# Maxima of attention scores for two heads at once on row tiles of 64 partitions, and the value projection as one product of 128 columns

## What is computed

```python
h = h + attn(layernorm(h))        # 64 images, 861 tokens, 4 heads of 16
h = h + ffn(layernorm(h))         # a shared MLP and the two best of four experts

# attn
q, k, v = heads(x @ Wq.T + bq), heads(x @ Wk.T + bk), heads(x @ Wv.T + bv)
attn = softmax(einsum('bhnd,bhmd->bhnm', q, k) * 16 ** -0.5)
out = einsum('bhnm,bhmd->bhnd', attn, v)
```

## Time and profile before

| | us |
|---|---|
| median of 3 runs | 5057.14 (5054.25 to 5059.23) |
| profiled execution | 5066.99 |
| its span, first to last instruction | 5065.2 |
| PE busy in the span | 4809.6 |
| DVE busy in the span | 3530.6 |
| ACT busy in the span | 2990.7 |

### The profile page before, as it was taken

The page is one execution under the profiler, slowest core; times in us unless marked ns, Lnnn a source line. Parts: engine busy times, 40 slices in busy tenths (PEclk is TensorE's granted clock), DMA queues, the critical chain, the costliest instruction groups (busy, mean ns, idle before and its releaser), DMA issues.

```text
span 5065.2 us, 81302 instructions
## 1 busy us (share of the span) xinstructions
PE 4809.6 (95%) x29710; PEld 3201.2 (63%) x29710; DVE 3530.6 (70%) x7660; ACT 2990.7 (59%) x6161; POOL 1272.2 (25%) x1169
## 2 busy tenths in 40 slices
PE   6699999999999999999999999999999999999997
PEld 5466666666666666666656666666666666666654
DVE  4477667777777777777677777777767677777774
ACT  0156566666566566566656556666656666656665
POOL 3122222222222222223222222222223222222221
PEclk8699999999999999999999999999999999999998
DMA  2433323333433332333332333332333333332220
GB/s 87 106 72 76 85 78 78 85 71 76 87 79 78 85 73 78 86 81 77 84 70 75 84 80 78 86 72 74 87 83 79 80 82 71 79 85 69 40 47 6
DMA packets 193397, 386.00 MB, mean 76 GB/s; under 512 B 74986, under 2 KB 118634, under 8 KB 193002
## 3 DMA queue, kind: packets, MB, share of 16 engines
q1 hardware_dynamic: 191978, 379.91, 33.3%
q10 hardware_dynamic: 1024, 0.89, 0.1%
HBM read 309.13 MB, written 109.26 MB: 83 GB/s over the span
## 4 chain that ended last, share of the span: by engine, by line
PE 55%; issue 23%; POOL 10%; DVE 6%; ACT 3%; DMA 2%; POOLq 0%; SPq 0%; ACTq 0%; DVEq 0%; another core or an unknown queue 0%
PE ps L1225 9%; PE ps L1204 8%; PE ps L1213 8%; PE ps L1257 8%; PE ps L1275 5%; PE ps L1248 4%; PE ps L1318 3%; DVE neg_max_halves L977 3%; POOL tokens L829 3%; POOL moe_T L824 2%; ACT probs L861 2%; PE ps L1339 2%; PE ps L364 1%; POOL nodes_T L806 1%; DMA image_rows<-image_by_row 1%
## 5 line engine op out<-in xcount | busy, mean ns | idle before, releaser
L977 DVE TENSOR_REDUCE neg_max_halves<-ps 123x1 f32<-123x432 f32 (+1 forms) x3584 | 2014.6, 597 | 602.6 <-PE ps L1225 592.9
L861 ACT ACTIVATE probs<-ps 123x432 f32<-123x432 f32 x3584 | 1684.0, 541 | 603.3 <-PE ps L1204 580.4
L1225 PE MATMUL ps<-k_stack,q_stack 96*123 96x432 f32 x3584 | 1302.3, 397 | 35.7 <-DMA k_stack<-qk_scratch 21.6
L1204 PE MATMUL ps<-q_stack,k_stack 97*123 97x432 f32 x3584 | 1246.8, 394 | 63.9 <-DVE neg_max_halves L977 22.1
L1225 PEld LDWEIGHTS ps<-k_stack,q_stack 96*123 96x123 f32 x3584 | 646.7, 188 | 431.6 <-issue 290.3
L1204 PEld LDWEIGHTS ps<-q_stack,k_stack 97*123 97x123 f32 x3584 | 642.8, 186 | 359.0 <-issue 96.2
L1213 PE MATMUL ps<-probs,v_and_one 123*32 123x432 f32 x7168 | 787.8, 553 | 14.0 <-ACT probs L861 14.0
L924 ACT ACTIVATE hidden<-ps,plain_w 128x432 f32<-128x432 f32 x640 | 400.2, 634 | 181.0 <-PE ps L1275 180.9
L1257 PE MATMUL ps<-adjacency,parts_hi 112*128 112x392 f32 x1344 | 466.1, 347 | 5.1 <-DVE parts_lo L999 4.1
L1257 PE MATMUL ps<-adjacency,parts_lo 112*128 112x392 f32 x1344 | 459.9, 342 | 0.0
L359 POOL COPY patch_columns<-image_rows 96x392 f32<-96x392 f32 x256 | 243.2, 978 | 845.0 <-PE ps L364 756.2
(11 more groups left out here) (157 smaller groups left out, 6115.3 us busy)
## 6 DMA issues: line engine op xcount, KB each, us to landing
image_rows<-image_by_row SPq DMA_DIRECT2D x256, 586.9 KB
q_stack<-qk_scratch SPq DMA_DIRECT2D x256, 216.0 KB, 7.9
k_stack<-qk_scratch SPq DMA_DIRECT2D x256, 216.0 KB, 9.3
image_by_row<-in_x SPq DMA_DIRECT2D x192, 196.0 KB
qk_scratch<-parts_hi SPq DMA_DIRECT2D x64, 432.0 KB, 2.5
qk_scratch<-parts_lo SPq DMA_DIRECT2D x64, 432.0 KB, 3.1
out<-tokens SPq DMA_DIRECT2D x64, 215.2 KB
tokens_next<-in_txt SPq DMA_DIRECT2D x64, 19.2 KB
```

Of the source, the lines that this page charges most:

```text
L861: act.activation(P[:, (g * 2 * NB + unit) % SLOTS, h, :], T[0:BLK, 0:HW], ACT.Exp, scale=SCALE).then_inc(free[r], 1)
L977: v.tensor_reduce(NM[:, qb * HEADS + h, half:half + 1], T[0:BLK, 0:keys], AX.X, ALU.max, negate=True).then_inc(free[r], 1)
L1204: mm = pe.matmul(T[0:BLK, 0:cn], KS[:, g % 2, h, kb * BLK:(kb + 1) * BLK], QS[:, g % 2, h, c0:c0 + cn], start=True, stop=True)
L1225: mm = pe.matmul(T[0:BLK, 0:cn], QS[0:SHIFT_ROW, g % 2, h, qb * BLK:(qb + 1) * BLK], KS[0:SHIFT_ROW, g % 2, h, c0:c0 + cn], start=True, st ...
```

## The change

- The query and key stacks of heads 0 and 1 stay in rows 0 to 63 (shift row 96). Those of heads 2 and 3 move to rows 64 to 127, with rows 0 to 63 zero but for their shift row, which is row 0.
- `mx` contracts over 64 rows at tile position (0, 0) for heads 0 and 1 and (64, 0) for heads 2 and 3. Four of them share one time in the list: heads h and h+2 of the first half of the keys, then h and h+2 of the second. The list has 14 such groups for each image in place of 56 single steps. The number of matmuls and of VectorE reductions is the same.
- `s` contracts over 97 rows for heads 0 and 1 and over 128 for heads 2 and 3.
- The stacks are filled by 16 transfers of two heads each, in place of 8 of four. The maxima's row goes out in two transfers, in place of one, each time.
- `v` has one product of 128 columns for each block (high and low weights side by side, `vsplit`), in two steps of 4 and 3 blocks, and VectorE adds bias and both parts in two additions for each step: four in place of one for each image.
- The table of times is changed in many places by up to a few hundredths of a period.

```diff
-STACK_PARTS = 8
+STACK_PARTS = 16
...
-        for h in range(HEADS):
-            for half in range(2):
-                out.append(("mx", g, qb, h, half))
-                out += due[:1] if half else []
-                due = due[1:] if half else due
+        for h in range(2):
+            out.append([("mx", g, qb, h + up, half) for half in range(2) for up in (0, 2)])
+            out += due[:1]
+            due = due[1:]
...
-MAX = ((-0.693, 0.158), (-0.638, 0.167))
+MAX = ((-0.691, 0.196), (-0.631, 0.174))
...
-VALUE = (-1.012, -0.998)
+VALUE = (-0.962, -1.061)
...
-                        copy, part, keys = n // 4, n // 2 % 2, n % 2
-                        src = scratch[b, part, keys].rearrange("h r c -> r h c")
-                        at = HD * (2 * part + copy) if keys else HD * (2 * copy + part)
+                        copy, part, keys, upper = n // 8, n // 4 % 2, n // 2 % 2, n % 2
+                        hs = slice(2 * upper, 2 * upper + 2)
+                        src = scratch[b, part, keys, hs].rearrange("h r c -> r h c")
+                        at = 64 * upper + (HD * (2 * part + copy) if keys else HD * (2 * copy + part))
...
-                        act.dma_start(QS[SHIFT_ROW:SHIFT_ROW + 1, g % 2, :, c].bitcast(F32), MR[:, c].bitcast(F32)).then_inc(mrow_dma[part], 16)
+                        for hs, at in ((slice(0, 2), SHIFT_ROW), (slice(2, 4), 0)):
+                            act.dma_start(QS[at:at + 1, g % 2, hs, c].bitcast(F32), MR[hs, c].bitcast(F32)
+                                          ).then_inc(mrow_dma[part], 16)
...
-                        v.tensor_tensor(
-                            VV[:, b, :, :, 0:HD],
-                            T[0:BLK, 0:NB * HID].rearrange("p (k h d) -> p k h d", h=HEADS, d=HD),
-                            row("bv").rearrange("p (h d) -> p h d", h=HEADS).unsqueeze(1)
-                            .to_broadcast([BLK, NB, HEADS, HD]), ALU.add).then_inc(free[r], 1)
+                        two = T[0:BLK, 0:kn * 2 * HID].rearrange("p (k a h d) -> p k a h d", a=2, h=HEADS, d=HD)
+                        bias = row("bv").rearrange("p (h d) -> p h d", h=HEADS).unsqueeze(1).to_broadcast([BLK, kn, HEADS, HD])
+                        done(v.tensor_tensor(VV[:, g % 2, k, :, 0:HD], two[:, :, 0, :, :], bias, ALU.add), st)
+                        need(st)
+                        v.tensor_tensor(VV[:, g % 2, k, :, 0:HD], two[:, :, 1, :, :], VV[:, g % 2, k, :, 0:HD], ALU.add
+                                        ).then_inc(free[r], 1)
...
-                        mm = pe.matmul(T[0:BLK, 0:cn], KS[:, g % 2, h, kb * BLK:(kb + 1) * BLK],
-                                       QS[:, g % 2, h, c0:c0 + cn], start=True, stop=True)
+                        k = SHIFT_ROW + 1 if h < 2 else 128
+                        mm = pe.matmul(T[0:BLK, 0:cn], KS[0:k, g % 2, h, kb * BLK:(kb + 1) * BLK],
+                                       QS[0:k, g % 2, h, c0:c0 + cn], start=True, stop=True)
...
-                        mm = pe.matmul(T[0:BLK, 0:cn], QS[0:SHIFT_ROW, g % 2, h, qb * BLK:(qb + 1) * BLK],
-                                       KS[0:SHIFT_ROW, g % 2, h, c0:c0 + cn], start=True, stop=True)
+                        at = 64 * (h // 2)
+                        mm = pe.matmul(T[0:BLK, 0:cn], QS[at:at + 64, g % 2, h, qb * BLK:(qb + 1) * BLK],
+                                       KS[at:at + 64, g % 2, h, c0:c0 + cn], start=True, stop=True, tile_position=(at, 0))
...
-                            for part in (WH, WL):
-                                mm = pe.matmul(T[0:BLK, k * HID:(k + 1) * HID], x_, wsplit(part, "v"),
-                                               start=part is WH, stop=part is WL)
+                    elif kind == "v":
+                        for k, at in blocks_of(st[2]):
+                            mm = pe.matmul(T[0:BLK, at * 2 * HID:(at + 1) * 2 * HID],
+                                           XS["a"][:, k * BLK:(k + 1) * BLK], vsplit[:, :], start=True, stop=True)
```

More of the change, by code:

```diff
@@ L746, in run @@
                 landed(stack_dma, 16, "stack")
-                landed(mrow_dma[0], 16, "mload", 0)
-                landed(mrow_dma[1], 16, "mload", 1)
+                landed(mrow_dma[0], 32, "mload", 0)
+                landed(mrow_dma[1], 32, "mload", 1)
             def end(n):
@@ L886, in run @@
                         act.wait_ge(full[r], n)
-                        counted(act, mrow_dma[part], row_no[part], ("mload", st[1] - 1, part), 16)
+                        counted(act, mrow_dma[part], row_no[part], ("mload", st[1] - 1, part), 32)
                         act.activation(blocked(MR[:, c0:c0 + cn]), pitched(T[0:HEADS, :], cn),
```

70 lines of the change are left out of this document (37 added, 33 removed).

## The result

| | before | after |
|---|---|---|
| median of the runs, us | 5058.2 (4 runs) | 5445.9 (5436.5 to 5451.9, 4 runs) |
| profiled execution, us | 5067.0 | 5440.4 |

The ratio is 1.0763, 95% interval 1.0740 to 1.0786: 7.6% slower. The forecast was 5013, with 8 chances in 10 between 4880 and 5150. It named slower as possible, through rival (b), at 5146; what came lies over four times as far from the kernel before as that.

What follows compares the result with a forecast made beforehand. It took TensorE's own work to bound the kernel, beside it VectorE emptying banks where maxima are dense; 5067 - 154 + 98 + 8 + 4 = 5023 us profiled, 5013 for the median, 8 in 10 between 4880 and 5150.

Steps and rivals of the forecast that it cites:

- rival (b): At reuse of a group's four banks, VectorE's bursts decide: waits at the upper end, +231 us, 5146 us, slower; chance 0.25.
- Products side by side, 0.40 for a group: In the maxima's products, row tiles run in pairs, 0.40 us for four instead of 0.80: 353 us saved.
- the switches, 0.19 each: On TensorE, each change of tiling costs 0.19 us, array running empty plus exposed first load: 1301 of them, 247 us lost.
- (a): On TensorE, the first load after a switch is hidden and banks cost nothing new: 4834 us; chance 0.17.
- (c): In the maxima's groups, loads of row tiles go one after another: +97 us, 5110 us; chance 0.08.
- (d): In the maxima's groups, row tiles run one after another, so the 353 us saving is lost: 5268 us; chance 0.05.
- Value projection, -48: In the value products, 7 products per step group cost as much each as 14 did: 48 us saved; VectorE's additions counted nothing.
- What is late next, the banks, +98, at most +231: At the PSUM banks, groups fill four of six, so TensorE waits for VectorE's reductions: 309 us replacing 211, at most 442.
- My walk through the list: Over the changed order of steps, 584 of 896 groups ask for banks too early, by 0.53 us on average: 309 us.
- TensorE's gain of 154: TensorE's own work falls by 353 for paired products, less 247 for switches, plus 48 for value products: 154 us.
- Transfers, +8 and +4: Doubled issues for the maxima's row on ScalarE's queue cost 8 us (0 to 76); extra stack transfers cost 4 us.
- The cover that I named for the stacks: Stack transfers land in 8.9 us and start some 20 us ahead of the first `mx`: hidden, except for the first image.

Runs made afterwards that it cites:

- full rows in fours: The kernel before with only the maxima's products put in groups of four, on full rows (96) without row tiles: 5574.3 us, ratio 1.1013.

## Why the prediction was wrong, by its steps

- **Products side by side, 0.40 for a group, and the switches, 0.19 each: right.** From the changed kernel with short reductions and exponentials, two untiled products, a group and two more, where nothing is waited for:

```profile
3017.32 0.47 PE L1291 MATMUL ps<-x_stack_moe,split_hi 128*128 128x432 f32 x1
3017.63 0.35 PE L1291 MATMUL ps<-x_stack_moe,split_lo 128*128 128x432 f32 x1
3017.91 0.66 PE L1241 MATMUL ps<-k_stack,q_stack 64*123 64x432 f32 x4
3018.51 0.46 PE L1291 MATMUL ps<-x_stack_moe,split_hi 128*128 128x432 f32 x1
3018.80 0.36 PE L1291 MATMUL ps<-x_stack_moe,split_lo 128*128 128x432 f32 x1
```

  and its loads:

```profile
3017.91 0.29 PEld L1241 LDWEIGHTS ps<-k_stack,q_stack 64*123 64x123 f32 x4 [0.29 <-issue]
3018.50 0.19 PEld L1291 LDWEIGHTS ps<-x_stack_moe,split_hi 128*128 128x128 f32 x1 [0.30 <-issue]
```

  From 3017.63 to 3018.80 are 1.17 us, where my terms give 0.29 + 0.30 + 0.29 + 0.30 = 1.18 and six starts without tiles 1.20. Inside a group, the medians over the 754 that start at full clock are 3 ns from the first to the second start, 294 to the third and 3 to the fourth. This rules out (a), (c) and (d), each by its own sign: the first load after a switch is exposed, loads of row tiles don't go one after another, and the tiles do run together. It also says how little an isolated group had to give: 0.03 us. The count of switches holds too: the trace of the changed kernel has 1271 more changes of tiling than the one before, for the prediction's 1301.
- **The rule of the Trainium skill that a load overlaps a matmul only on other row groups** ("TensorE: Matmul & The Clock Gate", Part 3) gave the same time as (c). (The same Part of the Trainium skill also names loads into a background weight buffer as ones that go ahead.) The row of four loads is against it as a rule here: each load lasts 0.19 us and all four are over 0.29 after the first began, so the last began by 0.10, in the first pair's time and on its rows. **The other rule**, that tiling doesn't speed up the emptying of PSUM ("TensorEngine Tiling (Array Packing)", Performance Considerations), points the right way: with 32 keys for each reduction the loss is 10 us, with 432 it is 389. But full rows in fours, where nothing is sped up, lose 10.1%: what decided is the order in which the banks are filled, and not the speed of the tiles.
- **Value projection, -48: the products right, the rest wrong.** TensorE spends 48 us less on them. But "I set it to nothing, what hides it is that VectorE is idle 30% of the span" is an average over the span, and the additions stand where reductions are awaited. At worst I had 58 us; alone they cost 158 more than the term.
- **What is late next, the banks, +98, at most +231: the step that failed.** The place, the mechanism and its owner were right, and are rival (b). The size was not: waits for reductions of 442 us at most, and 724 measured in the same ten groups (762 over all). The step failed twice. My walk through the list gave 309 us with VectorE doing nothing else; the waits of the changed kernel's trace in which VectorE does nothing but reductions sum up to some 425. And I multiplied by 1/0.70 as if VectorE's other work were spread evenly between reductions. It comes in part as chains, such as 4.1 us of three layer norm steps ahead of one group in the stretch shown: 338 of the 762 us are waits in which VectorE has other work (54 of 213 before), and 258 us are waits longer than 1.5 us (2 before). A burst on four of six banks meets a chain with two banks in hand, where single steps had five by my own count. Chains aren't the whole of it: with full rows in fours 152 of 507 us are such waits, 28 us are longer than 1.5 us, and the loss is 10.1% all the same. An upper bound should at least have held the longest chain ahead of a group, less those two banks' time; that chain stands in the order of instructions quoted ahead of the prediction. No run tests that bound.
- **ScalarE: nearly missing from the sum.** TensorE's waits for it rose by 96 us in the changed kernel, and with short reductions by 181, where TensorE's gain of 154 doesn't appear in the time. Of the 96, the transfers alone make 59 and fours on full rows 11; how much is the same burst on ScalarE is open.
- **The clock: missing from the sum.** I priced a wait at its length. 240 us more at half clock are up to 120 us of the 373 between the two spans; in the run of fours with full rows up to 232 of 507.
- **Transfers, +8 and +4: mis-sized.** Together 43 us by the ratio, over half of my upper end of 76 for ScalarE's issues. The cover that I named for the stacks held; ScalarE's idle time before `s`, again an average, was not enough of a cover.

Together: 373 us between the spans, plus 154 that TensorE's own work should have given, are 527 to explain. The clock is up to 120, the transfers about 45 (part of it the clock's), and the rest are the waits for banks, whose sums rose by 549 for reductions and 96 for ScalarE and are partly hidden under running matmuls. The exact split between waits and clock isn't settled: no run held the clock fixed while the waits changed, and the runs with the old table and with a long step behind each group show how far the sum of waits and the time can part. No run here that computes everything beat the kernel before. What is shown is that the order in fours loses 10% by itself, and that the loss goes when the reductions are short.

## What to carry to other kernels

Before work is packed into bursts for one engine, count the buffers that a burst leaves free, and lay them against the longest chain of other work that can stand ahead of the burst on the engine that empties them, not only against that engine's mean load. (No run here tested this as a rule of sizing.) Idle time of an engine, averaged over the span, hides nothing by itself: look at what it does in the microsecond in which the new work comes. Then allow for what the clock may take after each new wait.

## What was not expected of the hardware

- Waits of about 2 us in an otherwise busy stretch were followed by half clock. In the stretch shown, 1.91 us of waiting, a granted clock of 0.50 from 3054 to 3060, and `pv` at 3.11 us in place of 1.66. Four additions in a row on VectorE, with waits of 0.3 to 0.6 us on TensorE around them, were followed by it too. Between kernels that differ by little the time at half clock ranged from 157 us (the changed kernel with 32 keys for each reduction) to 1049 (with the old table of times).
- Half clock doesn't always grow with the waits. With short exponentials beside short reductions, the kernel before has shorter waits for ScalarE and VectorE together than with short reductions alone (397 us against 545), and more half clock (344 us against 177). Why is open.
- Two 64-row tiles start 3 ns apart, the next pair some 294 ns later, of which 0.10 is a load that didn't run ahead, and each change of tiling costs 0.19 us in all: as much as one whole product of 432 columns.
- Transfers of half the size landed in half the time (4.2 and 4.7 us at 108 KB, for 7.9 and 9.3 at 216 KB).
